# Half of the softmax sums of a decoder kernel, added up on GpSimd instead of by ScalarE's running sum

## The reference

```python
def _softmax(x, axis=-1):
    return jax.nn.softmax(x, axis=axis)
```

## Time and profile before

| | |
|---|---|
| median of 3 runs | 5704.05 us (5701.13 to 5717.39) |
| the profiled execution's own time | 5674.14 us |
| its span | 5672.6 us |
| PE busy | 5110.4 us (90%) |
| ACT busy | 3051.5 us (54%) |
| DVE busy | 2829.6 us (50%) |
| POOL busy | 23.6 us (0%) |
| mean granted TensorE clock | 0.962 |

### The profile page before, as it was taken

The page is one execution under the profiler, slowest core; times in us unless marked ns, Lnnn a source line. Parts: engine busy times, 40 slices in busy tenths (PEclk is TensorE's granted clock), DMA queues, the critical chain, the costliest instruction groups (busy, mean ns, idle before and its releaser), DMA issues. The chain is left out here.

```text
span 5672.6 us, 81045 instructions
## 1 busy us (share of the span) xinstructions
PE 5110.4 (90%) x27990; PEld 2613.1 (46%) x27990; DVE 2829.6 (50%) x6564; ACT 3051.5 (54%) x11252; POOL 23.6 (0%) x34
## 2 busy tenths in 40 slices
PE   7999988889799998888889999888898999989889
PEld 4444445544444444554344444455434444445443
DVE  5255555562525555556253545555625255555562
ACT  5444565564544456656454445665645444466564
POOL 0000000000000000000000000000000000000000
PEclk9989999999999999999999989999999999999999
DMA  1100000000010000000001000000000100000000
GB/s 37 41 6 6 18 18 12 5 1 15 25 41 6 6 21 18 9 5 1 19 25 37 6 6 20 18 9 5 1 19 22 41 6 6 23 16 9 5 1 19
DMA packets 22511, 85.93 MB, mean 15 GB/s; under 512 B 2512, under 2 KB 3024, under 8 KB 21968
## 3 DMA queue, kind: packets, MB, share of 16 engines
q1 hardware_dynamic: 22096, 80.58, 4.4%
HBM read 78.47 MB, written 2.10 MB: 14 GB/s over the span
## 5 line engine op out<-in xcount | busy, mean ns | idle before, releaser
L1051 ACT ACTIVATE work<-bank,rowmax 128x128 f32<-128x128 f32 (+1 forms) x4096 | 1395.1, 395 | 306.7 <-DVE rowmax L1366 305.9
L1051 ACT ACTIVATION_READ_ACCUMULATOR work<-bank,rowmax 128x1 f32 x4096 | 989.1, 244 | 0.0
L1366 DVE TENSOR_REDUCE rowmax<-bank 128x4 f32<-128x512 f32 (+2 forms) x1152 | 610.8, 578 | 458.8 <-PE bank L677 346.6
L694 PE MATMUL bank<-ident,work 128*128 128x128 f32 (+1 forms) x4096 | 658.2, 289 | 134.5 <-DVE probsT L1425 101.9
L542 PE MATMUL bank<-mask_causal,identb 128*128 128x512 bf16 x2368 | 676.3, 394 | 40.1 <-issue 28.7
L694 PEld LDWEIGHTS bank<-ident,work 128*128 128x128 f32 (+1 forms) x4096 | 488.6, 148 | 349.1 <-DVE probsT L1425 172.5
L1164 ACT ACTIVATE work<-bank,small 128x512 f32<-128x512 f32 x544 | 371.8, 688 | 490.1 <-PE bank L883 490.1
L910 PE MATMUL bank<-work,slot 128*128 128x512 f32 x1344 | 611.7, 592 | 0.0
L1621 DVE SCALAR_TENSOR_TENSOR part<-bank,small,sq 128x512 f32<-128x512 f32 x192 | 144.1, 751 | 785.0 <-PE bank L910 775.4
L1425 DVE COPY probsT<-bank 128x512 f32<-128x512 f32 (+2 forms) x832 | 479.6, 600 | 68.7 <-PE bank L694 64.9
L677 PE MATMUL bank<-km,q 32*128 32x512 f32 (+2 forms) x1792 | 426.2, 570 | 19.3 <-ACT work L1051 11.9
(11 more groups left out here) (266 smaller groups left out, 6226.6 us busy)
## 6 DMA issues: line engine op xcount, KB each, us to landing
slot<-in_w_stream SPq DMA_DIRECT2D x68, 512.0 KB, 3.4
slot<-in_w_stream SPq DMA_DIRECT2D x32, 768.0 KB, 3.9
slot<-in_w_stream SPq DMA_DIRECT2D x32, 384.0 KB, 3.1
small<-in_w_small SPq DMA_DIRECT2D x1, 2288.0 KB, 9.0
x<-in_x SPq DMA_DIRECT2D x8, 256.0 KB, 3.6
out<-x SPq DMA_DIRECT2D x8, 256.0 KB, 2.0
ctx<-in_ctx SPq DMA_DIRECT2D x8, 77.0 KB, 3.4
```

The lines of the kernel that those rows point to most:

```text
L694: ins = nc.tensor.transpose(b[0:nk, j * P:(j + 1) * P], probs[t % 2][:, r, j, 0:nk], ident[:])
L1051: ins = nc.scalar.activation(probs[t % 2][:, r, j, 0:nk], banks.where(("scores", n, c, s, r))[:, j * nk:(j + 1) * nk], ACT.Exp, bias=rowma ...
L1366: V.tensor_reduce(m[:, 4 * r:4 * r + J], banks.where(("scores", n, c, s, r))[:, 0:J * nk] .rearrange("p (j k) -> p j k", j=J), AX_X, ALU.m ...
```

## The change

In the stages with 16 heads and no relative term (L0_attn, L1_xattn, L2_attn, L2_a1, L2_a2, L3_ffn) the exponentials of blocks 0 and 1 are taken without accum_out. GpSimd waits for "probs" of block 1, adds the second half of the columns of those 8 heads to the first half, halves again until one column is left, and writes the 8 sums to the same columns of expsum. Each add waits for the one before it ("pool_step"); the last gives "pool_sum", for which VectorE's reciprocal now waits as well. With 77 keys the halving goes 32, then the 13 that remain, then 16, 8, 4, 2, 1. L3_attn and the linear stages are as before. The reduction order of the sums is another, and nothing else of what is computed changes.

```diff
+POOL_SUMS = (0, 1)
...
+        ptmp = sb("ptmp", [P, len(POOL_SUMS), 4, 64])
...
+        def summed_by_pool(st, r):
+
+            return not st["linear"] and not st["rel"] and r in POOL_SUMS
...
                                 for j in range(J):
-                                    ins = nc.scalar.activation(probs[t % 2][:, r, j, 0:nk],
-                                                               banks.where(("scores", n, c, s, r))[:, j * nk:(j + 1) * nk],
-                                                               ACT.Exp, bias=rowmax[t % 2][:, 4 * r + j:4 * r + j + 1],
-                                                               accum_out=expsum[t % 2][:, 4 * r + j:4 * r + j + 1])
+                                    out = probs[t % 2][:, r, j, 0:nk]
+                                    raw = banks.where(("scores", n, c, s, r))[:, j * nk:(j + 1) * nk]
+                                    top = rowmax[t % 2][:, 4 * r + j:4 * r + j + 1]
+                                    if summed_by_pool(st, r):
+                                        ins = nc.scalar.activation(out, raw, ACT.Exp, bias=top)
+                                    else:
+                                        ins = nc.scalar.activation(out, raw, ACT.Exp, bias=top,
+                                                                   accum_out=expsum[t % 2][:, 4 * r + j:4 * r + j + 1])
...
                             dve.wait_ge(*have("probs", (n, c, s, blocks(st)[-1])))
+                            if summed_by_pool(st, 0):
+                                dve.wait_ge(*have("pool_sum", (n, c, s)))
...
+                        if summed_by_pool(st, 0):
+                            for t, (c, s) in enumerate(items):
+                                last = POOL_SUMS[-1]
+                                pool.wait_ge(*have("probs", (n, c, s, last)))
+                                if t >= 2:
+                                    pool.wait_ge(*have("wide", (n, *items[t - 2])))
+                                if summed:
+                                    pool.wait_ge(*have("pool_sum", summed[-1]))
+                                summed.append((n, c, s))
+                                values, nk = probs[t % 2][:, 0:last + 1, :, :], st["nk"]
+                                width = 64 if nk == P else 32
+                                total = ptmp[:, 0:last + 1]
+                                link(nc.gpsimd.tensor_tensor(total[:, :, :, 0:width], values[:, :, :, 0:width],
+                                                             values[:, :, :, width:2 * width], ALU.add))
+                                if nk > 2 * width:
+                                    rest = total[:, :, :, 0:nk - 2 * width]
+                                    link(nc.gpsimd.tensor_tensor(rest, rest, values[:, :, :, 2 * width:nk], ALU.add))
+                                while width > 2:
+                                    width //= 2
+                                    link(nc.gpsimd.tensor_tensor(total[:, :, :, 0:width], total[:, :, :, 0:width],
+                                                                 total[:, :, :, width:2 * width], ALU.add))
+                                out = expsum[t % 2][:, 0:4 * (last + 1)].rearrange("p (r j) -> p r j", j=4).unsqueeze(3)
+                                nc.gpsimd.tensor_tensor(out, total[:, :, :, 0:1], total[:, :, :, 1:2], ALU.add
+                                                        ).then_inc(*made("pool_sum", (n, c, s)))
                         if st["wipes"]:
```

More of the change, by code:

```diff
@@ L1675, in _, with link @@
                 def _(pool):
+                    linked, summed = [0], []
+                    def link(ins):
+                        linked[0] += 1
+                        ins.then_inc(*made("pool_step", linked[0]))
+                        pool.wait_ge(*have("pool_step", linked[0]))
                     def mha(st):
                         n = st["name"]
+                        if summed_by_pool(st, 0):
[22 more added lines that the diff above has]
+                                                        ).then_inc(*made("pool_sum", (n, c, s)))
                         if st["wipes"]:
```

## The result

The changed kernel takes 5754.33 us (median of 9 runs, 5715.72 to 5770.64), the kernel before 5693.44 us in the same comparison (9 runs): 1.01 times as long, 95% interval 1.0077 to 1.0123. It is 61 us slower where 26 us faster was forecast. The profiled execution spans 5744.5 us, 72 more than before.

The account below looks back on a forecast made before the run. Items were taken to wait mostly for VectorE and TensorE, not ScalarE. Gains of 3.2 + 3 x 0.74 + 0.6 - 0.3 + 0.65 = 6.4 us a group, 25.6 us in four groups, gave 5678 us, range 5655 to 5742.

Parts of the forecast that it names:

- the one that puts the copy first: L0_attn and L2_attn: spread's copy starts 0.13 us after block 1, ahead of GpSimd's first add with its 0.23 us hand-over.
- the right rival: L0_attn and L2_attn: first add holds the port, copy waits about 1.2 us an item; 32 us slower net, chance 0.10.
- The chain of adds: GpSimd's seven dependent adds per item: 4.95 us, 4.05 with 77 keys, bounded between 2.9 and 6.5 us.
- Late sums: Rival: adds end too late for the reciprocal, at stage ends and in L1_xattn and L3_ffn; 33 us slower, chance 0.17.
- L1_xattn: Alternation of long and short items goes, 0.37 us an item, 2.2 us a group, plus 0.74 at the stage end.
- the 0.7 of its end: End of L2_attn: ScalarE's last copy and what follows come 0.74 us earlier, of which 0.6 us a group was counted.
- its last reciprocal is late and nobody waits: Stage ends: last reciprocal waits for the adds, 1.7 us late, 0.8 with 77 keys; 1.2 us of lateness costs nothing.
- L2_a1: No such ScalarE copy at this stage's end, so no gain, and 0.3 us of loss behind the late reciprocal.
- L3_ffn: TensorE and VectorE alone need about 6.24 us an item, so 0.16 of 6.40 is gained, 1.0 us a group.
- L2_a2: Memset of vm no longer delays a mid-stage spread's copy (1.35 us), new collision at the end; net gain 0.65 us a group.
- The 0.7 us that I had counted against it there: End of L2_a2: the moved memset starts just ahead of the spread's last copy, counted as a loss of 0.7 us.

Follow-up runs that it names:

- kernel 1: Changed kernel with one wait moved: GpSimd's first add of an item also waits for the spread's copy of the item before; 5653.4 us, 0.994 of the kernel before.
- kernel 8: Changed kernel with the moved wait, and GpSimd's wipes of vm held until the last spread's copy of L2_a2; 5638.71 us, 0.993 of the kernel before.
- 14: Kernel with all read-outs and GpSimd's adds unused, plus a 2.9 us VectorE stall in each group at L0_attn; 5689.95 us, 1.0009 of the kernel before.
- 4: Kernel before, no GpSimd adds, with some 1.15 us of VectorE delay ahead of the spread's copy in L0_attn and L2_attn; 5816.3 us, 1.0224 of before.
- 11: Changed kernel with the moved wait in every stage but L0_attn, which keeps the old wait; 5702.95 us, 1.0032 of the kernel before.
- 12: Changed kernel with the moved wait in every stage but L2_attn, which keeps the old wait; 5693.39 us, 1.0017 of the kernel before.
- kernel 3: Kernel before with all read-outs kept, plus GpSimd's adds written to a tile that nobody reads; 5718.75 us, 1.0058 of the kernel before.

## Why the prediction was wrong

**The step that failed** is the one that puts the copy first: "GpSimd works through the waits for probs, wide and pool_sum first, and 0.23 us was its hand-over the earlier trace rows, so the copy should be first." The margin was read rightly: 0.13 us from the end of block 1 to the copy, 0.10 measured. But GpSimd starts 0.08 us after block 1 in all 192 items. The 0.23 us were a hand-over between two of its own instructions in the setup; with the waits for wide and pool_sum long met and only one event outstanding it is 0.08, and so it is between the adds. Why the setup's was longer is not shown. So the add was 0.02 us ahead, and the copy waited for its end: 1.32 us for 0.23, items of 8.13 us for 7.04. I had the right rival with the right price (1.2 us an item, 58 us, 32 slower net) and gave it 0.10, on a margin of 0.1 us and one row from the setup. At an equal clock its 58 stands against the 59 us between the changed kernel and kernel 1, its 32 against 30 measured, and kernel 1 shows that the order is its cause.

**The chain of adds** was mis-sized on the safe side: 4.95 us predicted, 3.92 measured (3.07 for 77 keys, 4.05 predicted). An element costs (1268 - 205) / 504 = 2.1 ns, near the 2.2; nearly all of the difference is the six hand-overs, 0.08 us each for 0.23. Late sums were never near; in L0_attn the sums are ready 4.0 us ahead of the reciprocal.

**The gains came mostly as predicted or better.** Exponentials without read-outs are 0.25 us apart (eight in 2.18 us). L1_xattn lost its long items but for one of 5.8 us: from first exponential to first exponential the seven distances sum to 40.2 us where they were 42.5, and the stage with its end is 3.1 us shorter (2.9 predicted). L2_attn in kernel 1 is 94.1 us for 94.8, the 0.7 of its end; its last reciprocal is late and nobody waits, as forecast. L2_a1 gains 0.3 where a loss of 0.3 was said. L3_ffn has 6.33 us an item where 6.33 and 6.50 alternated and 6.24 was forecast. Its distances from the second item on are 0.8 us shorter in kernel 1's first group (1.0 predicted). In the changed kernel they are 0.8 us longer than before in every group, since one of them is 7.76 us for 6.12 at a lower clock: there this gain did not show.

**L2_a2** gained 3.1 us a group where 0.65 was counted. 1.35 are the item without a collision (7.96 to 6.61). The rest comes behind the last item, where the clock of the stage is 1.00 for 0.99; it is no sure gain, for in kernel 1 the stage takes 124.5 to 127.6 us from group to group. The collision did move to the stage end, as predicted:

```profile
1041.25 1.80 POOL L1726 MEMSET vm<- 128x2048 f32 x1
1041.41 0.25 DVE L1407 RECIPROCAL inverse<-expsum 128x16 f32<-128x16 f32 x1 [0.71 <-POOL expsum L1720]
1041.70 1.63 DVE L1411 COPY spread<-inverse 128x512 f32<-128x512 f32 x1
```

The 0.7 us that I had counted against it there were nothing (kernel 8). All gains together are 29 us at an equal clock in kernel 1, against 25.6 predicted.

**The clock** was no term of the sum, and it is half of the measured loss. What is shown: it is not GpSimd's work (14). A longer wait can bring it down inside the stage (4), and each colliding stage costs 0.003 to 0.005 (11, 12), which fits. In the profiled execution 16 us are lost to it inside the colliding stages, and most of the rest in stages that the change leaves as they were (32 us in L1_0 to L1_3 and L3_attn). But kernel 3 lost 0.008 with no late copy and had most of it back with a short stall, so I can't say how much of the changed kernel's 31 us belongs to the collisions and how much to where its stages happened to fall. That stays open; it would take many versions of the changed kernel, each shifted by another stall.

## What to carry to other kernels

Before work goes to GpSimd, list what VectorE does between SBUF and SBUF while it runs, and who starts first. If the margin is a tenth of a microsecond either way, treat the collision as likely, or make the order certain: one wait for an event that is due anyway turned 61 us of loss into 33 of gain here. Where the clock varies between runs, compare kernels at an equal clock too; otherwise a lower clock in stages that the change does not touch is taken for its direct effect.

## What the hardware showed that I had not expected

An add of GpSimd that waits for ScalarE alone starts 0.08 us after it, 192 times of 192, and that was enough to be ahead of a copy that came 0.10 us after the same event. Of VectorE's operations beside an add, a copy and a two-operand maximum from SBUF to SBUF wait (1.32 and 1.38 us), a reciprocal from SBUF to SBUF does not (0.24 us for 16 columns at 58.18, started behind an add; 0.94 for 128), nor do a copy out of PSUM (0.67 to 0.69) and a product with an operand in PSUM (0.28). And in one kernel of three, four stalls of 2.9 us in a program of 5.7 ms came with a mean clock 0.006 higher and a time 29 us shorter.
